# GpSimd waits for each group of nine gathers to land before it issues the next nine

## What is computed

```
qkv = depthwise3x3(groupnorm(x) @ qkv_w + qkv_b)
for g in range(8):                       # head
    off  = 18 offsets per pixel, from q, plus a fixed grid of radius 2*g + 1
    k[g] = bilinear(k_map[g], off) * mask      # 9 samples of 32 channels per pixel
    v[g] = bilinear(v_map[g], off) * mask
attn = softmax(q . k / sqrt(32))         # over the 9 samples
x = x + (sum over samples of attn * v) @ proj_w + proj_b
# layer 1, on the 4096 pixels of each image as tokens
t = t + attention(layernorm(t))          # 8 heads of 32, convolutions of width 3 in and out
t = t + mixture of 8 experts(layernorm(t))
```

## Time and profile before

| | |
|---|---|
| runs (us) | 12311.74, 12329.67, 12356.55; median 12329.67 |
| profiled execution: span, first to last instruction (no other time of it is given) | 12255.1 |
| PE busy | 8279.2 (68%) |
| DVE busy | 5175.9 (42%) |
| ACT busy | 3780.5 (31%) |
| POOL busy | 4967.5 (41%) |
| gathers, L661 | 4608, first at 523.4, last at 9645.9 |
| mean granted TensorE clock | 0.808 |

### The profile page before, as it was taken

How to read it: one execution, slowest core, us unless ns; L and a number is a source line. 1 busy time by engine, 2 the same in 40 slices (tenths; PEclk the granted TensorE clock), 3 DMA queues, 4 the chain that set the end, 5 groups by cost and what they waited for, 6 DMA issues and landing times. The chain is left out here.

```text
span 12255.1 us, 95913 instructions
## 1 busy us (share of the span) xinstructions
PE 8279.2 (68%) x31522; PEld 4334.5 (35%) x31522; DVE 5175.9 (42%) x10029; ACT 3780.5 (31%) x5495; POOL 4967.5 (41%) x4864
## 2 busy tenths in 40 slices
PE   6544656445663576666667765666666888998699
PEld 3522323332332233332333332333333333443366
DVE  6522334344443454444434443444444435663333
ACT  2100003001441144332434442324324563553122
POOL 1255564555445454454445554544554200000222
PEclk9776877666886688886878887778878898999799
DMA  3833233555332433333332334333343212113321
GB/s 133 281 93 89 92 124 111 185 194 158 95 91 86 128 99 97 93 100 107 94 97 89 103 91 121 110 114 99 98 123 95 70 45 74 41 45 80 123 71 49
DMA packets 658541, 1283.55 MB, mean 105 GB/s; under 512 B 189043, under 2 KB 398218, under 8 KB 643408
## 3 DMA queue, kind: packets, MB, share of 16 engines
q0 software_dynamic: 234240, 639.57, 17.4%
q1 hardware_dynamic: 405392, 562.58, 15.4%
q10 hardware_dynamic: 18432, 75.51, 1.5%
HBM read 1003.44 MB, written 278.91 MB: 105 GB/s over the span
## 5 line engine op out<-in xcount | busy, mean ns | idle before, releaser
L661 POOL DMA_INDIRECT sa_slot<-s_table,sa_rec x4608 | 4710.2, 1022 | 4902.7 <-DVE sa_vals L759 2347.2
L1651 DVE CUSTOM_DVE_ANT_0 a_above<-a_late,a_above 128x512 f32<-128x512 f32 x1600 | 1103.8, 690 | 3209.4 <-remote 1358.3
L1592 ACT ACTIVATE a_above<-a_diff 128x512 f32<-128x512 f32 x1600 | 956.4, 598 | 3189.2 <-DMA s_kd<-p_diff_lo 1408.5
L1558 PE MATMUL a_ctx<-a_p,a_v 128*64 128x512 f32 x6400 | 1714.9, 660 | 95.3 <-issue 95.2
L1583 ACT ACTIVATE a_p<-a_s 128x1024 f32<-128x1024 f32 x1600 | 1628.7, 1020 | 322.4 <-remote 163.3
L1503 PE MATMUL a_late<-a_k,a_q 96*128 96x512 f32 x1600 | 859.6, 537 | 838.5 <-DVE a_pair_max L1651 446.0
L1491 PE MATMUL a_diff<-a_kd,a_q 96*128 96x512 f32 x1600 | 773.9, 484 | 848.1 <-issue 460.6
L1541 PE MATMUL a_s<-a_q,a_k 98*128 98x512 f32 x3200 | 1110.2, 432 | 43.8 <-ACT a_p L1583 35.6
L816 PE MATMUL sa_sums<-keep_ident,sa_vals 128*128 128x128 f32 x4608 | 741.2, 308 | 565.8 <-issue 360.4
L1503 PEld LDWEIGHTS a_late<-a_k,a_q 96*128 96x128 f32 x1600 | 330.7, 207 | 1810.8 <-issue 1206.9
L816 PEld LDWEIGHTS sa_sums<-keep_ident,sa_vals 128*128 128x128 f32 x4608 | 640.4, 161 | 693.2 <-issue 445.6
(11 more groups left out here) (280 smaller groups left out, 8224.9 us busy)
## 6 DMA issues: line engine op xcount, KB each, us to landing
sa_slot<-s_table,sa_rec POOLq DMA_INDIRECT x4608
s_table<-t_rows ACTq DMA_DIRECT2D x64, 1024.0 KB, 7.5
a_q<-s_q SPq DMA_DIRECT2D x480, 128.0 KB, 2.6
s_part<-a_o SPq DMA_DIRECT2D x160, 256.0 KB
t_qwin<-s_dwq SPq DMA_DIRECT2D x64, 512.0 KB
t_kvwin<-s_dwkv SPq DMA_DIRECT2D x64, 386.0 KB
a_kd<-s_kd SPq DMA_DIRECT2D x384, 64.0 KB
a_o<-s_part SPq DMA_DIRECT2D x96, 256.0 KB, 2.7
```

What stands on the lines that cost most here:

```text
L661: pool.indirect_dma_start(out=self.slot[g][:, k, :, :, :].rearrange("p c a n -> p (c a n)"), out_offset=None, in_=self.s["table"][n // TIL ...
L1558: mm = pe.matmul(self.ps_ctx[i * 2 * HD:(i + 1) * 2 * HD, :], self.v_and_ones(run.head, kb), self.p[slot % P_SLOTS][:, i * CHUNK:(i + 1) * ...
L1592: act.activation(self.above[slot % n][:, :], self.ps_diff, ACT.Relu).then_inc(self.diff_got, 1)
L1651: dve.tensor_tensor_reduce(above, self.ps_late, above, 1.0, LOWEST, ALU.add, ALU.max, self.pair_max[:, t, j:j + 1]).then_inc(self.late_got, 1)
```

## The change

Ahead of each group but the very first, GpSimd also waits until all nine gathers of the group before it, in whichever slot they went to, have landed. The order of the gathers, their number and everything on the other engines are as before.

```
--- before
+++ after
@@ -657,6 +657,9 @@
             pool.wait_ge(self.tile_in[n % 2], 32 * (n // 2) + 32)
         if n > 0:
             pool.wait_ge(self.values_made, G * (n - 1) + g + 1)
+        if G * n + g > 0:
+            before = G * n + g - 1
+            pool.wait_ge(self.gathered[before % G], 16 * K * (before // G + 1))
         for k in range(K):
             pool.indirect_dma_start(
                 out=self.slot[g][:, k, :, :, :].rearrange("p c a n -> p (c a n)"), out_offset=None,
```

## The result

| | before | change |
|---|---|---|
| runs, median (us) | 12341.88 (12311.74 to 12356.55, 4 runs) | 11004.41 (10980.76 to 11008.84, 4 runs) |
| ratio | | 0.8912, 95% interval 0.8896 to 0.8928 |
| profiled execution (us) | span 12255.1 | 10980.76, span 10979.0 |
| mean granted TensorE clock | 0.808 | 0.85 |

Faster by 10.9%, where 6.3% was forecast (11548 us) and the range was 10650 to 12480. Which chip it is turns out to be half of the story: on chip D the same change is 13% **slower**. Chip A first. (Of experiment 3's four runs on chip B one, at 11092.98 us, was in a slower state, 1.8% above the fastest, and is left out of the time and ratio there.)

The account below looks back on a forecast made before the run. No engine was full; GpSimd's gathering was taken to stall attention beside sampling. Median 12330, less 840 for half the stalls returned, plus 58 for landing waits, gave 11548 us; range 10650 to 12480.

Parts of the forecast that it names:

- What bounds the kernel: Attention beside sampling: no engine is full; something present only while GpSimd gathers slows it, not sampling's arithmetic; 1678 us lost.
- The stalls, -840: Attention beside sampling: pauses between groups give back half of the 1678 us lost, -840 us.
- The pause, +1.7 us: GpSimd inside a run: the next group starts at the landing, 1.7 us later than after the last issue.
- some 400: Sign of being right: some 400 idle times of 2.0 us before GpSimd's gathers, ended by the landing.
- What hides this is the slack of the slots: Runs of four groups: 16 us of slot slack covers the added 3 x 1.7 = 5.1 us.
- +58: Groups whose landings VectorE already waits for: 34 new pauses of 1.7 us paid in full, +58 us.
- The items per us: Sign in attention beside sampling: at least 0.31 items per us; halfway from 0.257 to 0.386 is 0.32.
- half of 1358.3: Sign of being right: "remote" waits before the attention instruction down to half of 1358.3 us.
- Rivals 3 and 4: rival 3; and balance: stalls give back about what series and longer runs cost, 12293 to 12367 us; chance 0.09.
- rival 3: Gather runs of four: the stall lasts as long as the run, each 5.1 us longer; up to 13041 us; chance 0.10.
- Rival 2: Stalls aren't the gathers' doing, or don't mind a 2 us pause; only landing waits pay: 12388 us; chance 0.13.
- The rule against the change: Skill's rule to wait late on a DMA, against 511 immediate waits; by it alone the sum would be +58 us.

Follow-up runs that it names:

- experiment 3: Kernel before plus a wait ahead of each group for eight of the last group's nine gathers, not the ninth: 10912.07 us on B, ratio 0.8740.
- experiment 5: Kernel before plus a 128x48 memset on GpSimd ahead of each gather: 9687.54 us on C, ratio 1.0023; 12447.89 us on E, ratio 0.9934.
- experiment 6: Kernel before with eight of the nine gathers of every group left out (wrong values): 8953.17 us on C, ratio 0.9264.
- experiments 2 and 3: Kernel before plus the landing wait ahead of every second group only: 11362.99 us on B, ratio 0.9075; and experiment 3.
- the five memsets: Kernel before plus five 128x256 memsets in sequence on GpSimd between groups, no landing wait: 10590.77 us on B, ratio 0.8481; 10430.81 on C, 1.079.
- experiment 1: Kernel before plus a wait ahead of each group for the landing of the group before the last: 12522.06 us on B, ratio 1.0017.
- experiments 6 and 7: experiment 6; and kernel before with gathered rows of 64 floats in place of 256 (wrong values): ratios 1.0051, 1.0019, 1.0007 on C, D, F.

## Why the prediction was right, and where it was not

The account can now be made without a share chosen by hand. Spans: 12255.1 us before on A; 9689.0 us without the stall, from experiment 5 on C, whose ratio to the kernel before is 1.002; 10979.0 us for the change. So the change **takes away some 2570 us of stall and adds some 1290 us of pauses**, -1276 in all. The split compares two chips, so it is an estimate. The second term is measured on one chip too: 10976.92 - 9674.92 = 1302 us on D, and 511 pauses longer by 2.8 - 0.30 = 2.5 us are 1278.

| stretch, us | before, A | experiment 5, C | change, A | change, D |
|---|---|---|---|---|
| groups 0 to 77 | 1209 | 965 | 1168 | 1169 |
| groups 100 to 141 | 668 | 504 | 656 | 673 |
| groups 295 to 391, with attention | 1798 | 1236 | 1469 | 1466 |
| all of attention beside sampling | 5632 | 3943 | 4721 | 4732 |
| after the last gather | 2608 | 2561 | 2562 | 2534 |

(From the starts and ends of the gathers in the timelines; the fourth row sums groups 142 to 191, 216 to 283, 295 to 391, 400 to 415, 424 to 467 and 476 to 511.)

- **What bounds the kernel: right.** That the loss lies where GpSimd gathers and is not sampling's arithmetic holds: the chips differ there and hardly anywhere else. It isn't the whole cause. On C, D and F the same gathers bring no stall (they do set the pace there: experiment 6 gained 7.4%), so there are two conditions, gathering in one piece and a chip of the one kind. One trace could not show the second.
- **The stalls, -840: right in sign, mis-sized twice.** The bound for those stretches was sound: 1678 us, and between A and C they differ by 5632 - 3943 = 1689. But the share was all, not half; the change takes 11004 us on A and 10977 on D, 27 us apart, and in the two traces A takes longer only after the last gather (2562 against 2534). And stretches outside rows 4 held some 880 us more (2570 - 1689), 244 of them in groups 0 to 77, where I had left 60 us.
- **The pause, +1.7 us: it is 2.5.** The step took it that GpSimd restarts at the instant at which VectorE does, 2.03 us behind the last issue. It restarts 2.27 us behind in the row above and 2.8 us in the median. The waits ended by the landing are there, 465 in place of "some 400".
- **"What hides this is the slack of the slots", +58: this step failed.** The slack of 16 us was there because the stall kept VectorE and TensorE late. With the stall gone they catch up with GpSimd, and every pause is on the path: on C, where there is no stall, GpSimd has no slack even without the pauses (experiment 5). The text had the figures, a floor of 52 us by GpSimd against 52 us of attention undisturbed, and called it the best case only. With pauses of 2.8 us the median group starts 14.7 us after the one before it, so four take 59 us, above attention's 52: GpSimd is the bound. The term was +1290 us, rows 2's 35 landing waits became 205, and the wait of L710 for a landing grew to 11.4 us in a series, not 10.7. (The +58 also rests on a miscount that changes little: the series as listed hold 39 waits, not 35; in the trace they have 9, 12, 2, 4 and 8. That moves the term by under 7 us.)
- **The items per us** came out at 0.325, near the 0.32 that was to show half a relief. The check could not tell "half of the stall left" from "no stall, and GpSimd the pace-maker". The second was seen in two other rows: GpSimd's waits for values down to 102.9 us, and "remote" at 129.2 where half of 1358.3 was forecast.
- **That the time fell in the range is partly luck.** The relief was taken some 1730 us too small and the cost some 1230 too small, and the two errors offset each other; and the chip was of the stalling kind. On D the measured ratio is 1.134, above the whole range (12480 / 12330 = 1.012).
- **How short a pause is enough.** The reading from the earlier trace rows, that a pause before the collapse prevents what one in it doesn't mend, agrees with every run. The table has the pause, in the rows shown above, beside an estimate of the stall that is left: the time on a stalling chip less that on one without (for experiments 2 and 3 the latter is 9670 us plus the added pauses, 255 x 2.4 and 511 x 1.1 us; on the change that way is 24 us short, on the five memsets 150 us over; by experiment 3's median pause of 1.56 us its two estimates would be 10310 and 600).

| pause between groups | time with stall, us | without, us | stall left, us |
|---|---|---|---|
| 0.30 (before) | 12501 (B) | 9663 (C) | 2838 |
| 0.30, memsets in the gaps | 12448 (E) | 9688 (C) | 2760 |
| 2.74, every second group | 11363 (B) | 10280, estimate | 1080 |
| 1.43 | 10912 (B) | 10230, estimate | 680 |
| 2.1, memsets | 10591 (B) | 10431 (C) | 160 |
| 2.8 (the change) | 11004 (A) | 10977 (D) | 27 |

The "remote" waits before the attention instruction need no such estimate and fall in the same order on the stalling chips: 1358.3 us before and 1515.2 in experiment 1, then 1013.4 (every second group), 599.3 (experiment 3), 317.9 (memsets) and 129.2 (the change). No trace from C, D or F has a "remote" wait.

- **The rivals.** Rivals 3 and 4 fall: runs got longer and TensorE didn't die in them (none of the 40 windows on A under 7 of 10 us). On D the change is slower, as rival 3 has it, but not by its mechanism: GpSimd's pace costs it, not a stall that lasts. Rival 2 in its second half (the stall doesn't mind a pause) falls. Its first half, that the stall is not the gathers' doing, wasn't tried by taking gathers away on a stalling chip; that it answers to GpSimd's pauses and ends with the last gather speaks against it. The Trainium skill (SBUF — State Buffer, "Who interferes with whom"), by which a DMA never contends with a compute engine for SBUF and TensorE and ScalarE wait for nobody there, would give no stall. C looks like that (0.373 items per us beside gathers, 0.371 without), E doesn't (0.245 beside, and TensorE at 0.00 of 10 us). Whether the stall has to do with SBUF at all no run shows.
- **The rule against the change.** The Trainium skill (DMA: Bandwidth & Descriptors, "Rules for kernel authors") says to wait late on a DMA. The wait that goes against it was priced at +58 us; on D, without the stall, it cost 1302 us, so there the rule holds, and on A it did not.

**No version won everywhere.** On the stalling chips the five memsets are the best measured, 0.848 against 0.891 for the change (on two chips); on the others the kernel before is, and the memsets cost 7.9% (one run on C), the change 13.4% (on D). Of these chips A, B and E stalled, C, D and F did not, so which kernel to use depends on where the kernel will run. A pause only in runs where GpSimd is ahead was not tried.

**Open:** what differs between the chips, and whether it stays with them, since each was met in one session; whether bytes or descriptors of the gathers matter, since experiments 6 and 7 never met a stalling chip; and by what path a gathering GpSimd holds up TensorE, VectorE and ScalarE together. The kernel before was not profiled on a chip without the stall; experiment 5 stands in for it.

## What to carry to other kernels

Before you price a wait against slack, ask what the slack is made of: if the stall that you are removing made it, it goes with the stall, and the floor of the next engine (here 59 us against 52) is the new time. Compute that floor for the forecast, not only for the best case. And where a trace shows waits that no engine ends, repeat the kernel before on other chips before you tune against them: here the same two kernels stand at 0.891 and at 1.134. To size a pause, try one that does nothing but pass time, and make it longer until the gain stops.

## What the hardware showed that I had not expected

- The kernel before takes 12330 to 12535 us on some chips and 9663 to 9679 us on others, each within 0.6% over 4 to 13 runs. The traces from A, B and E show engines idle together while GpSimd gathers; those from C, D and F have no "remote" wait. Beside attention the core on C moves 140 GB/s, that on E 90.
- A stall of 2.8 ms went to 0.16 ms (12501 and 10591 us on B, 9663 and 10431 on C) when GpSimd stopped gathering for 2.1 us after each 11 us. At the same mean pace, a pause of 1.4 to 1.6 us every group beat one of 2.7 to 3.1 us every second group by 451 us.
- A memset of 128x48 between two gathers is nearly free: 0.15 us in the 0.30 us gap, a gather each 1.26 us for 1.25.
- GpSimd takes up its queue later than VectorE does after the same landing: 0.74 us in the median of the 205 groups on which VectorE waited in the change, 0.23 in the rows shown.
